# Node phase 2 of a four-layer graph network: one gated product fewer, hats stored by component, a shorter projection, and a doubled row added behind the hats

## The reference, cut to what matters

```python
ps, pv = _eq_lin(ns, nv, proj_ws, proj_bs, proj_wv)          # 64x64 on scalars, 32x32 on each component
x = node_input + _merge(ps, pv)
s2, v2 = _eq_ln(x, ln2_w0, ln2_b0, ln2_w1)                   # the "hats": normalised scalars and vectors
a0 = node_attr[:, :1]
fs, fv = _eq_lin(s2, v2, f1_ws, f1_bs, f1_wv)                # 64 -> 128 + 64 scalars, 32 -> 64 vectors
fs = fs * a0
fv = fv * a0[:, :, None]
sc = jax.nn.silu(fs[:, :M0])                                 # M0 = 128
fv = fv * jax.nn.sigmoid(fs[:, M0:])[:, :, None]             # 64 gates, one for each of 64 vectors
os_, ov = _eq_lin(sc, fv, f2_ws, f2_bs, f2_wv)
return x + _merge(os_ * a0, ov * a0[:, :, None])
```

## Time and profile before

| | us |
|---|---|
| three runs of the kernel | 6612.5, 6617.95, 6619.99 |
| their median | 6617.95 |
| the profiled execution, its own time | 6613.59 |
| its span in the trace | 6611.8 |
| of it node phase 2, from its first instruction to the last store | about 4392 to 5445 |
| PE busy over the span | 5254.7 (79%) |
| POOL busy over the span | 4467.9 (68%) |
| DVE busy over the span | 4395.2 (66%) |
| ACT busy over the span | 2710.7 (41%) |

### The profile page before, as it was taken

How to read it: one execution, slowest core, us unless ns; L and a number is a source line. 1 busy time by engine, 2 the same in 40 slices (tenths; PEclk the granted TensorE clock), 3 DMA queues, 4 the chain that set the end, 5 groups by cost and what they waited for, 6 DMA issues and landing times. The chain is left out here.

```text
span 6611.8 us, 124233 instructions
## 1 busy us (share of the span) xinstructions
PE 5254.7 (79%) x28474; PEld 4008.9 (61%) x28474; DVE 4395.2 (66%) x14949; ACT 2710.7 (41%) x5812; POOL 4467.9 (68%) x4689
## 2 busy tenths in 40 slices
PE   8899966679997997999455344459999989999676
PEld 6565656646666995777122233347777777777665
DVE  3566658844445886887677322238888887777788
ACT  5333347734443663444000000015555544443566
POOL 8688856658886887664577688856666657887222
PEclk9899989989998998999788666679999999999899
DMA  8566667736666764554311344432222224554665
GB/s 320 118 125 121 123 163 220 222 93 130 129 127 170 230 211 123 161 156 144 87 33 33 101 74 76 76 58 96 97 97 97 97 75 93 87 85 70 213 224 187
DMA packets 592231, 850.69 MB, mean 129 GB/s; under 512 B 220783, under 2 KB 340383, under 8 KB 587567
## 3 DMA queue, kind: packets, MB, share of 16 engines
q1 hardware_dynamic: 409646, 693.63, 33.0%
q0 software_dynamic: 182400, 154.98, 17.0%
HBM read 469.52 MB, written 377.54 MB: 128 GB/s over the span
## 5 line engine op out<-in xcount | busy, mean ns | idle before, releaser
L1138 POOL DMA_INDIRECT xg<-x,gidx x600 | 618.7, 1031 | 249.8 <-issue 184.3
L326 POOL DMA_INDIRECT agg<-summed,cidx x400 | 643.2, 1608 | 193.7 <-issue 114.0
L2015 PE MATMUL pc_a<-msg_a,same_a 128*128 128x168 f32 x1000 | 259.7, 446 | 416.3 <-ACT summed_a L2002 358.6
L2015 PEld LDWEIGHTS pc_a<-msg_a,same_a 128*128 128x128 f32 x1000 | 246.8, 302 | 429.9 <-issue 303.4
L399 DVE TENSOR_TENSOR pr<-pf,ws 128x512 f32<-128x512 f32 x200 | 138.3, 691 | 521.9 <-PE pf L486 382.3
L1149 POOL DMA_INDIRECT agg<-summed,cidx x200 | 324.2, 1621 | 78.9 <-issue 58.5
L1961 POOL DMA_INDIRECT agg<-summed_a,cidx_a x200 | 317.8, 1589 | 70.7 <-issue 59.7
L1312 ACT ACTIVATE ob<-po 128x416 f32<-128x416 f32 (+1 forms) x400 | 201.5, 504 | 359.7 <-PE po L1389 188.0
L1881 PE MATMUL pm_m<-arow_m,ones_m 128*128 128x512 bf16 x400 | 152.1, 470 | 234.4 <-DVE top_m L1828 232.4
L515 PEld LDWEIGHTS pc<-ob,same 128*128 128x128 f32 x2000 | 278.6, 191 | 81.4 <-issue 81.4
L2197 POOL TENSOR_TENSOR rs_n<-ve_n,wsb 128x4 f32<-128x4 f32 x98 | 98.7, 1007 | 337.8 <-DVE nm_n L2185 337.8
(11 more groups left out here) (350 smaller groups left out, 17944.6 us busy)
## 6 DMA issues: line engine op xcount, KB each, us to landing
ar_n<-agg SPq DMA_DIRECT2D x194, 322.0 KB
agg<-zero SPq DMA_DIRECT2D x50, 768.0 KB
ar_n<-agg SPq DMA_DIRECT2D x97, 384.0 KB
agg<-zero SPq DMA_DIRECT2D x50, 672.0 KB
ar_n<-agg SPq DMA_DIRECT2D x97, 336.0 KB
agg<-zero_h SPq DMA_DIRECT2D x25, 1288.0 KB, 5.4
agg<-zero SPq DMA_DIRECT2D x50, 644.0 KB
x<-xn_n SPq DMA_DIRECT2D x97, 324.0 KB, 2.7
```

The costliest lines, as they stand in the source:

```text
L326: pool.indirect_dma_start(agg, bass.IndirectOffsetOnAxis(ap=cidx[r][:, t:t + 1], axis=0), summed[u][:, t, :], None, compute_op=ALU.add).th ...
L1138: pool.indirect_dma_start(xg[s][r][:, t, 0:XR], None, x, bass.IndirectOffsetOnAxis(ap=gidx[s][r][:, t:t + 1], axis=0)).then_inc(gathered[r ...
L2015: last = pe.matmul(pc[:, t, 0:W], same[u][:, s, t * P:(t + 1) * P], msg[u][:, s, :], start=(s == t), stop=(s == T - 1))
```

## The change

It has four parts.

1. `first_product` has three products, not four. The hats' vector numbers are stored by component (all first components, then all second, then all third). Columns 65 to 96, the first component, thereby fall into the block with the scalars, `hts`, and `pf[1]` gives the 64 gates and the 64 vectors of one component at once. `pf[2]` gives the other two components. The weights go to other rows and columns, `f1p` is added and built into `f1s` by a fourth small product ahead of the pipeline.
2. The gates stand on 64 partitions only. `tg` needs them on 128, so `activate` runs the tanh twice over 64 partitions. `gated` takes `gvb` first, now from `pf[1]`, on the upper 64 partitions.
3. `project` has `pb` first with 160 columns, then `pa` with 64, where both had 160.
4. `twice` waits for `hat_ok` of its own chunk, so that the POOL adds the doubled row behind the hats. The POOL's order stays.

```diff
@@ @block.tensor, ahead of the pipeline
-            pe.wait_ge(scaled, 4)
+            pe.wait_ge(scaled, 5)
...
-            pe.matmul(pf[0][:, 0:2 * P], wt("e64"), wt("f1b"), start=False, stop=True).then_inc(b_ps, 1)
+            pe.matmul(pf[0][:, 0:2 * P], wt("e64"), wt("f1b"), start=False, stop=False)
+            pe.matmul(pf[0][:, 0:2 * P], wt("ident"), wt("f1p"), start=False, stop=True).then_inc(b_ps, 1)
@@ project
-                        pe.matmul(pk[:, t, 0:D], ata[:, t * P:(t + 1) * P], wt("pa"), start=True, stop=False)
-                        last = pe.matmul(pk[:, t, 0:D], atb[:, t * P:(t + 1) * P], wt("pb"), start=False, stop=True)
+                        pe.matmul(pk[:, t, 0:D], atb[:, t * P:(t + 1) * P], wt("pb"), start=True, stop=False)
+                        last = pe.matmul(pk[:, t, 0:S0], ata[:, t * P:(t + 1) * P], wt("pa"), start=False, stop=True)
@@ first_product
-                for g in range(2):
-                    pe.matmul(pf[2 + g][:], wt("f1v")[:, g * P:(g + 1) * P], htv[:], start=True, stop=True).then_inc(f_ps, 1)
+                pe.matmul(pf[2][:], wt("f1v"), htv[:], start=True, stop=True).then_inc(f_ps, 1)
@@ activate
-                a.activation(tg[:], pf[1][:], ACT.Tanh, scale=0.5).then_inc(act_ok, 1)
+                a.activation(tg[64:P], pf[1][0:64], ACT.Tanh, scale=0.5).then_inc(act_ok, 1)
+                a.activation(tg[0:64], pf[1][0:64], ACT.Tanh, scale=0.5).then_inc(act_ok, 1)
@@ gated
-                v.wait_ge(act_ok, 2 * c + 2)
+                v.wait_ge(act_ok, 3 * c + 3)
                 v.wait_ge(o_ps, due(2 * (c - 1)))
-                v.wait_ge(f_ps, 4 * c + 3)
+                v.wait_ge(f_ps, 3 * c + 3)
+                v.scalar_tensor_tensor(gvb[u][64:P], tg[64:P], 1.0, pf[1][64:P], ALU.add, ALU.mult).then_inc(gv_ok, 1)
                 v.scalar_tensor_tensor(gva[u][:], tg[:], 1.0, pf[2][:], ALU.add, ALU.mult).then_inc(gv_ok, 1)
-                v.wait_ge(f_ps, 4 * c + 4)
-                v.scalar_tensor_tensor(gvb[u][0:64], tg[0:64], 1.0, pf[3][0:64], ALU.add, ALU.mult).then_inc(gv_ok, 1)
@@ hats
-                v.tensor_tensor(hat[u][:, :, 65:HW], x1[u][:, :, S0:D], rs1[u][:, 1, :].unsqueeze(2).to_broadcast([P, T, V3]), ALU.mult).then_inc(hat_ok, 1)
+                v.tensor_tensor(hat[u][:, :, 65:HW].rearrange("p t (c u) -> p t u c", c=3), x1[u][:, :, S0:D].rearrange("p t (u c) -> p t u c", c=3),
+                                rs1[u][:, 1, :].unsqueeze(2).unsqueeze(3).to_broadcast([P, T, V1, 3]), ALU.mult).then_inc(hat_ok, 1)
@@ twice
                 pool.wait_ge(y_ok, due(T * (c - 3)))
+                fence(pool)
+                pool.wait_ge(hat_ok, 2 * (c + 1))
                 fence(pool)
                 pool.tensor_tensor(xx[r][:], x1[u][:], xr[r][:, :, 0:D], ALU.add).then_inc(xx_ok, 1)
```

More of the change, by code:

```diff
@@ L99 @@
 slot("avg", 128, 128)
-slot("pa", 128, 160)
+slot("pa", 128, 64)
 slot("pb", 128, 160)
@@ L108 @@
 slot("f1b", 1, 256)
-slot("f1v", 128, 256)
+slot("f1v", 128, 128)
+slot("f1p", 128, 256)
+slot("ln2p", 128, 1)
 slot("f2s", 128, 64)
@@ L2246, in node_phase_2 @@
         pk = ps("pk", [P, T, 256])
-        pf = each(4, ps, "pf", [P, B])
+        pf = each(3, ps, "pf", [P, B])
         scaled = sem("scaled")
@@ L2352, in first_product @@
                 pe.wait_ge(ht_ok, 2 * c + 2)
[L2353 removed]
+                pe.wait_ge(act_ok, 3 * c)
                 pe.wait_ge(gv_ok, 2 * c)
@@ L2400, in copy_rows @@
             def copy_rows(c, r, k, parts):
-                a.wait_ge(f_ps, 4 * c)
+                a.wait_ge(f_ps, 3 * c)
                 a.wait_ge(turned2, 2 * c + 1)
@@ L2430, in _ @@
             v.tensor_scalar(wt("f2va"), wt("f2va"), 0.5, None, ALU.mult).then_inc(scaled, 1)
-            v.tensor_scalar(wt("f2vb")[0:64], wt("f2vb")[0:64], 0.5, None, ALU.mult).then_inc(scaled, 1)
+            v.tensor_scalar(wt("f2vb")[64:P], wt("f2vb")[64:P], 0.5, None, ALU.mult).then_inc(scaled, 1)
+            v.tensor_scalar(wt("f1p"), wt("f1p"), wt("ln2p"), None, ALU.mult).then_inc(scaled, 1)
             for u in range(2):
-                v.memset(gvb[u][64:P], 0.0).then_inc(ones, 1)
+                v.memset(gvb[u][0:64], 0.0).then_inc(ones, 1)
                 v.memset(an[u][:, :, D:HW], 1.0).then_inc(ones, 1)
@@ L2436, in _ @@
             for u in range(2):
-                v.memset(gvb[u][64:65], 1.0).then_inc(ones, 1)
+                v.memset(gvb[u][0:1], 1.0).then_inc(ones, 1)
             def denominator(c, r, k, parts):
@@ L2725, in lay_out @@
     whole[D, 0:S0] = q["proj_bs"]
-    put("pa", 0, 0, whole[0:P])
-    put("pb", P - 33, 0, whole[P:D + 1])
+    put("pa", 0, 0, whole[0:S0, 0:S0])
+    put("pb", P - 97, 0, whole[S0:D + 1])
     put("ln2w", 0, 0, col(q["ln2_w0"]))
-    col3("ln2v", 32, q["ln2_w1"])
+    put("ln2p", S0 + 1, 0, col(q["ln2_w1"]))
+    for h in (64, 96):
+        put("ln2v", h, 0, col(q["ln2_w1"]))
     put("centre", 0, 0, np.eye(S0, dtype=np.float32) - np.float32(1.0 / S0))
     put("b0row", 0, 64, col(q["ln2_b0"]))
-    for h in (64, 128):
-        put("f1s", 0, h + 64, q["f1_ws"][:, 128:192])
-        put("f1b", 0, h + 64, row(q["f1_bs"][128:192]))
+    put("f1s", 0, 128, q["f1_ws"][:, 128:192])
+    put("f1b", 0, 128, row(q["f1_bs"][128:192]))
     put("f1s", 0, 0, q["f1_ws"][:, 0:128])
     put("f1b", 0, 0, row(q["f1_bs"][0:128]))
-    wide = np.zeros((V3, 192), np.float32)
     back = np.zeros((192, V3), np.float32)
     for k in range(3):
-        wide[k::3, k * 64:(k + 1) * 64] = q["f1_wv"]
         back[k * 64:(k + 1) * 64, k::3] = q["f2_wv"]
-    put("f1v", 32, 0, wide)
+    put("f1p", S0 + 1, 192, q["f1_wv"])
+    put("f1v", 64, 0, q["f1_wv"])
+    put("f1v", 96, 64, q["f1_wv"])
     put("f2s", 0, 0, q["f2_ws"])
-    put("f2va", 0, 0, back[0:128])
-    put("f2vb", 0, 64, back[128:192])
-    put("f2vb", 64, 0, row(q["f2_bs"]))
+    put("f2va", 0, 0, back[64:192])
+    put("f2vb", 64, 64, back[0:64])
+    put("f2vb", 0, 0, row(q["f2_bs"]))
     attr = np.zeros(((NC + 1) * P, T), np.float32)
```

6 lines of the change are left out of this document (3 added, 3 removed).

## The result

The changed kernel takes 6495.2 us (median of 4 runs, 6492.9 to 6501.8) where the kernel before takes 6615.9 us (4 runs, 6612.5 to 6620.0). The ratio is 0.9819, with a 95% interval from 0.9807 to 0.9831: 120.7 us less. The forecast was 6518 us, with a range of 6493 to 6553; the time is 23 us under the forecast and inside the range.

What follows compares the result with a forecast made beforehand. Two equally long chains, PE's and DVE's with the POOL, 10.22 us each, were taken to bound the kernel. Chunks falling from 10.45 to 9.45 us over 97 steps gave -97 us, hence 6518 us, range 6493 to 6553.

Steps and rivals of the forecast that it cites:

- Structure: In node phase 2, DVE's chain takes over as the bound, 0.2 us longer than PE's 9.22.
- Chain of DVE and POOL: From final sum to final sum, through the POOL's powers: claimed to fall from 10.22 to 9.42 us.
- the term of *`ve`: DVE's `ve`, before `x1`, would stand behind the POOL's shares: +0.3 us, bounds 0 and 0.6.
- scattered write: Vector hats stored by component, each number 32 places from the one before: +0.30 us on DVE's chain.
- Loop's head: Where the loop body begins anew: 0.03 us added to each chunk, half of PE's.
- PE's own branch: PE's branch at the loop's head: some 0.2 us, a quarter of it for each step, giving PE 9.22 us.
- PE's parts: Three products for four, -0.86 us, and the shorter projection, -0.19: PE's chain falls from 10.22 to 9.17 us.
- shorter projection: On PE, four projection products of 64 instead of 160 columns: -0.19 us, bounds 0 and -0.29.
- sign for the bound: PE's transposes would idle about 0.2 us in each chunk, with the hats named as releaser.
- rival 1: PE stays the bound at 9.22 us, as the scattered write or `ve`'s wait costs little: 6496 us; chance 0.25.
- Rivals 2, 3 and 4: Dearer scattered write, 6549 us, chance 0.23; hats still held, 6608, 0.02; write so dear it is slower, 6648, 0.03.
- rival 3: Vector hats still stand 1.2 us behind another POOL instruction in the doubled row's place: 6608 us; chance 0.02.

Runs made afterwards that it cites:

- e3: Changed kernel with the vector hats written in the old, adjacent order: 6755.4 us, where the kernel before took 6875.9 in its group; mean chunk 9.19 us.
- e5: Changed kernel with `ve` and `nm` made by tensor_reduce instead of tensor_scalar: 6729.3 us, mean chunk 9.25 us; the unedited changed kernel beside it took 6731.6.
- e8: Changed kernel with vector hats written in runs of 32 and read from `x1` at every third place: 6719.8 us, ratio 0.982, mean chunk 9.21 us.
- e4: Changed kernel without the projection's 64-column products (`pa`): 6761.2 us, where the kernel before took 6875.9 in its group; mean chunk 9.28 us.
- e6: Changed kernel with both the adjacent hats write and `ve` and `nm` by tensor_reduce: 6477.1 us, mean chunk 9.18 us.
- e2: Kernel before with only the fourth part added, the doubled row waiting for the hats: 6852.3 us, 23.6 less than the kernel before; mean chunk 10.19 us.
- e7: Changed kernel with `pa` run over all 160 columns again, the third part undone: 6510.1 us, 5.7 more than the changed kernel; mean chunk 9.44 us.
- e1: Changed kernel without its fourth part, the doubled row not waiting for the hats: 6901.5 us, 25.6 more than the kernel before; mean chunk 10.68 us.

## Why the prediction was right, and where it was off

**Structure: shown.** DVE's chain with the POOL's powers in it takes over as the bound. e3, e5 and e8 shortened it and the chunk got shorter; e4 took 0.7 us of work from PE and it hardly did. But it is narrow: DVE's 9.23 stands 0.10 above PE's 9.13, where I had 0.20 between them.

**Chain of DVE and POOL: 9.23 us, and I had 9.42.** By its steps in the timeline after:

| step | forecast | measured |
|---|---|---|
| final sum to `x1`, `ve` held | 2.93 + 0.30 = 3.23 | 3.17 |
| `x1` to last variance | 2.42 | 2.40 |
| powers, to scalar hats | 2.65 | 2.64 |
| scalar hats to vector hats | 0.34 | 0.35 |
| vector hats to final sum | 0.48 + 0.30 = 0.78 | 0.67 |
| all | 9.42 | 9.23 |

Nearly all of the 0.19 us lies between the start of the vector hats and `x1`: 0.78 + 3.23 = 4.01 forecast, 0.67 + 3.17 = 3.84 measured. It is a slip in the sum, in the term of *`ve`*. By my own figures `ve` starts 2.67 us behind the end of the hats and the shares end 3.0 us behind it, so that `ve` *lasts* 0.33 us. 0.17 of that was in the chain already, so that only 0.16 is *added*; I added 0.30. With 0.16 the chain would have been 9.28 us, the chunk 9.31 and the time about 14 us less, some 6504. The figures that went in were good: the shares end 4804.37 - 4801.36 = 3.01 us behind the hats.

The *scattered write* was right in size, 0.828 against 0.552 us, 0.28 more where I had 0.30. But it is no separate term of DVE's queue. While `ve` is held, the way goes from the *end* of the hats over the POOL's doubled row and shares to `x1`: 0.82 + 0.18 + 2.83 + 0.01 = 3.84. So the 0.28 counts in full (e3's step of 8.95), although the next final sum starts only 0.67 - 0.46 = 0.21 us later than in e6, where the write is adjacent (4809.40 to 4809.86). The hold takes up the difference: `ve` starts 4803.95 - 4801.36 = 2.59 us behind the end of the hats and not 2.67, and that is most of why it is lengthened by 0.44 - 0.17 = 0.27 and not by 0.16.

**Loop's head: 0.07 us, and I had 0.03.** The four steps from the power at 4807.22 take until this one:

```profile
4844.41 1.64 POOL L2542 TENSOR_TENSOR rsa_n<-var_n,wsb 128x8 f32<-128x8 f32 x1 [1.18 <-DVE var_n L2476]
```

They are 37.19 us, 9.30 each, 0.07 over 9.23. PE's own branch isn't the reason. I had put 0.2 us on it, but where PE sets the pace, in e6, its steps take 9.13, 9.13, 9.16 and 9.13 us, and in e2 10.19 each. Which of DVE's and POOL's instructions lose the 0.07 stays open. The mean over all 97 steps is 0.04 higher still, since filling and draining the pipeline count in it, as they did before (10.42 for four steps, 10.45 for the mean). So the forecast's 9.45 became 9.45 - 0.19 + 0.04 + 0.04 = 9.34.

**PE's parts.** The terms held. PE's chain was 10.22 and is 9.13, 1.09 less; I had 0.86 + 0.19 = 1.05. e7 gives the shorter projection 0.21 (I had 0.19, bounds 0 and 0.29), which leaves 0.88 for the fourth product. Only the time from the projection's start to the first product, 1.92 us, is less than my 1.99, and the 0.06 comes back in the product behind it.

**Signs.** Vector hats 0.83 us (0.85 forecast), `ve` 0.44 (0.3 to 0.5) ending with the shares, right. The gated products end 4808.97 - 4801.42 = 7.55 us behind the start of PE's transposes (7.4 forecast) and the scalar hats start at 8.00 (8.0), so the second tanh is hidden, as forecast. The sign for the bound was badly chosen. I said that PE's transposes would show 0.2 us of idle time with the hats as releaser. The rows print none in nearly all chunks; the wait is 0.10 us, and only the comparison with e6 brings it out. Read from that sign alone, rival 1 (PE stays the bound) would have looked right, the more so since its time, 6496, is the one measured. It was a coincidence: rival 1 had PE's chain at 9.22, and PE's is 9.13. So the forecast had the right bound, but its own time was further off than rival 1's.

**The rest of the 23 us.** The chunk, 9.34 for 9.45, gives 0.11 x 97 = 10.7 us. About 9 us lie in stages with unchanged code, in the profiled run. In the other two groups the changed kernel was 119.6 and 110.7 us under the one before, with the same mean chunk of 9.31; the 110.7 are about what the chunks give. So up to 10 us of this difference belong to no term of mine. In the profiled run 6 of them lie ahead of the stage (its first DVE instruction starts at 4386.56 instead of 4392.65). Between kernels with the same code there the stage's start moves by 12 us and more, as told above; what moves it stays open.

**Rivals 2, 3 and 4.** A chunk of 9.77 or more didn't come: the scatter costs 0.72 ns an element by duration, (828 - 552) / 384. Of the two figures of the Trainium skill (Vector Engine (DVE) Microarchitecture Reference, section Measured stream behaviour on trn2), which the prediction set beside this, the one for a destination that hops 4 KiB, an estimated 0.25 us more, is close to the measured 0.28. The one for steps of 24 words, 0.55 more, is far off for steps of 32 numbers. Nothing took the doubled row's old place, and rival 3 falls with it. e1 shows a way to be slower that I hadn't priced: the change without its last part.

## What to carry to other kernels

- Where two engines have chains of the same length, a change to one gives little (e2, 0.26 us a chunk of 1.1) or even loses (e1); measure the parts together, and price the pair by the next chain. Don't read the bound from "100% busy": take work from that engine and see whether the period moves.
- How long a held instruction lasts isn't what it adds: take off what it lasts when free (0.33 - 0.17 = 0.16 us here, not 0.30). And while it is held, its engine's chain runs through the queue of the engine that holds it, so the bound is read there, from the end of what released that queue.
- If an instruction must change the order of elements between float32 tiles, try it with runs in the write and the gaps in the read: reading at every third place cost 0.12 us more for 384 elements, writing in steps of 32 numbers 0.28.
